# Edge ranges packed two blocks to a register load, fewer register loads before the counting stage, and the number of earlier groups carried in registers

## The reference, cut to what matters

```python
src, dst = edges sorted by dst            # 21250 of them, 1250 nodes of 512 features
neigh = segment_sum(x[src], dst, 1250)    # layer 0: sum over the edges of each node
rst   = (1 + eps) * x + neigh
h     = relu(rst @ W1 + b1) @ W2 + b2 + x
x     = layernorm(x + h)
# then four blocks of attention over the same edges, each with conditional
# layernorms and a two-layer MLP; and a last layernorm
```

## Time and profile before

| | before |
|---|---|
| median of 3 runs | 1729.66 us (1729.47 to 1729.7) |
| the profiled execution's own time | 1729.81 us |
| its span (first to last instruction) | 1728.1 us |
| PE busy | 1708.2 us, 99% |
| start of the first count product | 15.36 us |
| start of the second group's products | 19.65 us |
| end of the counting stage | about 127.4 us |

### The profile page before, as it was taken

How to read it: one execution, slowest core, us unless ns; L and a number is a source line. 1 busy time by engine, 2 the same in 40 slices (tenths; PEclk the granted TensorE clock), 3 DMA queues, 4 the chain that set the end, 5 groups by cost and what they waited for, 6 DMA issues and landing times.

```text
span 1728.1 us, 32350 instructions
## 1 busy us (share of the span) xinstructions
PE 1708.2 (99%) x11894; PEld 1511.2 (87%) x11894; DVE 1214.8 (70%) x2229; ACT 802.9 (46%) x1325; POOL 555.1 (32%) x880
## 2 busy tenths in 40 slices
PE   8999999999999999999999999999999999999998
PEld 7998788889999888889998888899988888999887
DVE  7996559457786875477878673677776835778676
ACT  5668332136665331256663412466644123666531
POOL 1002613312334732023337340133363401333473
PEclk9999999999999999999999999999999999999999
DMA  4003311311111303121113122111131312112222
GB/s 136 1 1 150 116 49 44 127 71 40 47 59 38 96 32 129 40 67 45 47 32 105 48 89 80 47 46 62 32 100 36 109 41 79 34 46 62 70 92 73
DMA packets 64779, 113.08 MB, mean 65 GB/s; under 512 B 15318, under 2 KB 25686, under 8 KB 64640
## 3 DMA queue, kind: packets, MB, share of 16 engines
q1 hardware_dynamic: 64640, 111.22, 19.7%
HBM read 89.19 MB, written 22.00 MB: 64 GB/s over the span
## 4 chain that ended last, share of the span: by engine, by line
PE 98%; DVE 1%; issue 0%; DVEq 0%; DMA 0%; SPq 0%; ACT 0%; POOLq 0%; POOL 0%; ACTq 0%
PE ps L1565 61%; PE ps L1625 16%; PE ps L1720 7%; PE ps L1512 6%; PE ps L1542 3%; PE ps L1652 2%; PE ps L1666 2%; DVE masked_s L1272 1%; PE ps L1482 0%; DVEq L426 0%; PE ps L1581 0%; DMA idx_rows<-in_dst_dram 0%; PE ps L1576 0%; PE ps L1463 0%; DVE hot L1097 0%
## 5 line engine op out<-in xcount | busy, mean ns | idle before, releaser
L1256 DVE TENSOR_TENSOR pT<-ps,pT 128x640 fp32r<-128x640 f32 (+1 forms) x320 | 243.9, 804 | 153.9 <-ACT pT L1016 153.8
L1565 PE MATMUL ps<-yT,w 128*128 128x512 f32 (+1 forms) x1728 | 330.0, 352 | 0.0
L1016 ACT CAST pT<-ps 128x640 fp32r<-128x640 f32 (+1 forms) x320 | 202.4, 685 | 252.9 <-PE ps L1720 247.1
L1565 PEld LDWEIGHTS ps<-yT,w 128*128 128x128 f32 x1728 | 280.6, 189 | 44.8
L1565 PE MATMUL ps<-kh,q_parts 128*128 128x512 f32 (+3 forms) x1440 | 310.5, 360 | 5.4 <-DVE small L1272 5.4
L1565 PEld LDWEIGHTS ps<-kh,q_parts 128*128 128x128 f32 (+1 forms) x1440 | 243.0, 186 | 51.1 <-issue 3.7
L1565 PE MATMUL ps<-w,kh 128*128 128x512 f32 (+1 forms) x960 | 235.4, 396 | 0.0
L1625 PE MATMUL ps<-pT,v 128*128 128x256 f32 (+3 forms) x1600 | 215.6, 281 | 0.0
L953 ACT ACTIVATE s<-masked_s,small 128x1250 f32 (+1 forms) x156 | 211.2, 1354 | 0.0
L1565 PEld LDWEIGHTS ps<-w,kh 128*128 128x128 f32 (+1 forms) x960 | 173.7, 186 | 38.9 <-DVE q L1283 1.8
L1625 PEld LDWEIGHTS ps<-pT,v 128*128 128x128 f32 (+1 forms) x1600 | 200.3, 190 | 0.0
(11 more groups left out here) (189 smaller groups left out, 2534.4 us busy)
## 6 DMA issues: line engine op xcount, KB each, us to landing
mask<-mask_dram SPq DMA_DIRECT2D x24, 640.0 KB, 5.1
x_spill<-x SPq DMA_DIRECT2D x36, 256.0 KB
x<-x_spill SPq DMA_DIRECT2D x36, 256.0 KB, 4.3
rep<-rec_dram SPq DMA_DIRECT2D x64, 128.0 KB, 3.3
w_raw<-in_L_gnn_m_w_dram SPq DMA_DIRECT2D x8, 1024.0 KB, 6.4
mask_y<-mask_dram SPq DMA_DIRECT2D x12, 640.0 KB, 5.3
mask_dram<-mask_out SPq DMA_DIRECT2D x10, 640.0 KB, 2.9
w_l<-in_L_gnn_W_dram SPq DMA_DIRECT2D x2, 2048.0 KB, 13.5
```

The lines of the kernel that those rows point to most:

```text
L1016: nc.scalar.copy(pT[:, 0, turned_places(gh, half), k * P:k * P + R], turn_bank(half, R)).then_inc(p_high, 1)
L1256: nc.vector.tensor_tensor(pT[:, 1, places, k * P:k * P + R], turn_bank(half, R), pT[:, 0, places, k * P:k * P + R].bitcast(F32), ALU.subtr ...
L1565: mine = mm(to, left(a), right(b), start=first and n == 0, stop=final and n == 2)
```

## The change

Six edits. (1) `table` becomes int16, and one 32-bit register load brings the `first` and `quads` of two blocks; DVE and ACT load one value before the first group and four in one load after it, instead of four and then four and two. (2) The number of earlier groups is no longer computed by a product with a triangular matrix (`earlier`) and packed; each engine adds up the `quads` of the blocks that it has passed. (3) PE loads one value of `group_table` before the first group and two behind that group's products, and takes the largest number of groups from the same packed word. (4) POOL's packing waits for that largest number as well (`most_ready`). (5) ACT's first function-table load happens at the start, and its copies of `edge` wait for each half by itself. (6) The products of the bounds stand behind three tiles of x.

```diff
-        table = sb("table", [1, NT + 1], I32)
+        table = sb("table", [1, NT], mybir.dt.int16)
...
-        FIRST_LOAD, LATER_LOADS = range(0, 4, 4), range(4, NT, 4)
+        def load_edge_tiles(engine, first_pair, pairs):
+
+            _, packed = nc.values_load_multi_w_load_instructions(table[0:1, 2 * first_pair:2 * (first_pair + pairs)].bitcast(I32),
+                                                                 engines=(engine,), min_val=0, max_val=2 ** 30 - 1)
+            return list(packed)
+
+        def edge_tiles(eng, packed, j):
+
+            at = packed[j // 2] >> 16 if j % 2 else packed[j // 2]
+            first = eng.snap(at & (QUADS_AT - 1)).with_bounds(min_val=0, max_val=NE - 1)
+            quads = eng.snap((at >> 8) & 63).with_bounds(min_val=1, max_val=NE // HOT + 1)
+            return first, quads
+
+        def groups_before(eng, before, quads):
+            return eng.snap(before + quads).with_bounds(min_val=0, max_val=NT * (NE // HOT + 1))
...
-            act.wait_ge(consts, 4)
-            act.wait_ge(idx_t, 2)
+            act.wait_ge(consts, 6)
+            nc.scalar.copy(dst_gap[0:1, 0, 0:1], ident[0:1, 0:1])
             for a in range(2):
+                act.wait_ge(idx_t, 1 + 2 * a)
                 nc.scalar.copy(edge[:, a, 0:NE], ps[0:ET, a, 0:NE]).then_inc(edges_ready, 1)
...
-            chain(nc.vector.scalar_tensor_tensor(parts[:, 0, :], parts[:, 1, :], float(QUADS_AT), parts[:, 0, :], ALU.mult, ALU.add))
-            nc.vector.scalar_tensor_tensor(table[:, 0:NT], parts[:, 2, :], float(BEFORE_AT), parts[:, 0, :], ALU.mult, ALU.add).then_inc(tiles_s, 1)
-            chain(nc.vector.tensor_reduce(most[:], parts[:, 1, :], AX.X, ALU.max))
-            nc.vector.tensor_copy(group_table[:, 3:4], most[:]).then_inc(most_ready, 1)
+            nc.vector.scalar_tensor_tensor(table[:], parts[:, 1, :], float(QUADS_AT), parts[:, 0, :],
+                                           ALU.mult, ALU.add).then_inc(tiles_s, 1)
+            dve.wait_ge(groups_clear, 1)
+            nc.vector.tensor_reduce(four_groups[:, NT:NT + 1], parts[:, 1, :], AX.X, ALU.max).then_inc(most_ready, 1)
...
-            packed = load_edge_tiles(mybir.EngineType.DVE, FIRST_LOAD)
+            packed = load_edge_tiles(mybir.EngineType.DVE, 0, 1)
+            before = 0
             for j in range(NT):
-                first, quads, before = edge_tiles(dve, packed[j])
+                first, quads = edge_tiles(dve, packed, j)
                 if j == 0:
-                    hots(j, first, dve.snap(before * HOT))
-                    packed += load_edge_tiles(mybir.EngineType.DVE, LATER_LOADS)
+                    hots(j, first, 0)
+                    packed += load_edge_tiles(mybir.EngineType.DVE, 1, PAIRS - 1)
                 with dve.Fori(1 if j == 0 else 0, quads) as k:
                     hots(j, dve.snap(first + k * HOT), dve.snap((before + k) * HOT))
+                before = groups_before(dve, before, quads)
...
-            for t in range(4):
+            for t in range(3):
                 if t == 2:
                     pe.wait_ge(edges_ready, 2)
                 turn_x(t)
             pe.wait_ge(bounds_ready, 1)
-            for a, (value, onto) in enumerate(((0, ident), (1, ident), (1, earlier))):
-                mine = mm(ps[0:1, 5, a * NT:(a + 1) * NT], bounds[:, value:value + 1], onto[0:NT, 0:NT], start=True, stop=True)
+            for a in range(2):
+                mine = mm(ps[0:1, 5, a * NT:(a + 1) * NT], bounds[:, a:a + 1], ident[0:NT, 0:NT], start=True, stop=True)
...
+            load_groups(0, 1)
             before = 0
             for j in range(NT):
                 quads = pe.snap((fours[j // 4] >> 6 * (j % 4)) & 63).with_bounds(min_val=1, max_val=NE // HOT + 1)
-                count_block(j, j % 2, quads, before)
+                count_block(j, j % 2, quads, before, (lambda: load_groups(1, 2)) if j == 0 else None)
```

More of the change, by code:

```diff
@@ L338, in gnn_kernel @@
         tl_i32 = at("yp", 21504, "tl_i32", [NT, NE], I32)
-        parts = at("yp", 24896, "parts", [1, 3, NT])
-        most = at("yp", 25024, "most", [1, 1])
+        parts = at("yp", 24896, "parts", [1, 2, NT])
         four_groups = at("yp", 25056, "four_groups", [1, 12])
@@ L410, in gnn_kernel @@
         EXACT = 4096
-        CONSTS = 12
-        QUADS_AT, BEFORE_AT = 2 ** 8, 2 ** 14
+        CONSTS = 10
+        QUADS_AT, PAIR_AT = 2 ** 8, 2 ** 16
         TILES_DONE = 9
@@ L417, in x_piece @@
             return x_in_s[n], 32 if n == NG - 1 else 16
-        FIRST_LOAD, LATER_LOADS = range(0, 4, 4), range(4, NT, 4)
[L421 to L436, removed]
+        PAIRS = NT // 2
+        def load_edge_tiles(engine, first_pair, pairs):
[9 more added lines that the diff above has]
+            return eng.snap(before + quads).with_bounds(min_val=0, max_val=NT * (NE // HOT + 1))
         @block.sync
@@ L628, in _ @@
             nc.gpsimd.iota(edge_of_i[:], [[P, 2]], base=0, channel_multiplier=P).then_inc(consts, 1)
[L629 to L632, removed]
             nc.gpsimd.memset(minus_one[:], -1.0).then_inc(consts, 1)
@@ L668, in _ @@
             pool.wait_ge(parts_ready, 1)
+            pool.wait_ge(most_ready, 1)
             pool.sem_inc(passed)
@@ L851, in counts_copy @@
                                ).then_inc(counts_out, 1)
-            packed = load_edge_tiles(mybir.EngineType.Activation, FIRST_LOAD)
+            packed = load_edge_tiles(mybir.EngineType.Activation, 0, 1)
+            before = 0
             for j in range(NT):
-                first, quads, before = edge_tiles(act, packed[j])
+                first, quads = edge_tiles(act, packed, j)
                 dst_hots(j, first, before)
@@ L865, in _ @@
                 nc.scalar.copy(x_high[0:rows(j), j, :], x[0:rows(j), j, :]).then_inc(x_high_done, 1)
-            counts_copy(NT - 1, act.snap(before + quads))
+                before = groups_before(act, before, quads)
+            counts_copy(NT - 1, before)
             def rst_high_part(m, g):
@@ L1489, in _ @@
             pe.wait_ge(bounds_ready, 1)
-            for a, (value, onto) in enumerate(((0, ident), (1, ident), (1, earlier))):
-                mine = mm(ps[0:1, 5, a * NT:(a + 1) * NT], bounds[:, value:value + 1], onto[0:NT, 0:NT], start=True, stop=True)
+            for a in range(2):
+                mine = mm(ps[0:1, 5, a * NT:(a + 1) * NT], bounds[:, a:a + 1], ident[0:NT, 0:NT], start=True, stop=True)
             mine.then_inc(bounds_turned, 1)
-            for t in range(4, NT):
+            for t in range(3, NT):
                 if t == 7:
@@ L1496, in _, with count_block @@
                 turn_x(t)
-            def count_block(j, place, quads, before):
+            def count_block(j, place, quads, before, behind_first=None):
                 pe.wait_ge(counts_out, j + 1)
@@ L1516, in count_block @@
                 quad(before, True)
+                if behind_first:
+                    behind_first()
                 with pe.Fori(1, quads) as k:
@@ L1521, in _, with load_groups @@
             pe.wait_ge(group_step, 6)
-            pe.wait_ge(most_ready, 1)
-            _, fours = nc.values_load_multi_w_load_instructions(group_table[0:1, 0:4], engines=(mybir.EngineType.PE,), min_val=0,
-                                                                max_val=2 ** 24 - 1)
+            fours = []
+            def load_groups(a, n):
+                _, found = nc.values_load_multi_w_load_instructions(group_table[0:1, a:a + n], engines=(mybir.EngineType.PE,),
+                                                                    min_val=0, max_val=2 ** 24 - 1)
+                fours.extend(found)
+            load_groups(0, 1)
             before = 0
```

13 lines of the change are left out of this document (6 added, 7 removed).

## The result

| | before | after |
|---|---|---|
| median | 1729.66 us (1729.47 to 1731.34, 5 runs) | 1756.85 us (1756.66 to 1757.47, 5 runs) |
| profiled execution, its span | 1729.81, 1728.1 us | 1757.47, 1755.2 us |
| first count product | 15.36 us | 14.04 us |
| second group's first and third tile | 19.65, 20.85 us | 16.69, 18.40 us |
| start of the neighbour sums (end of the counting) | 127.29 us | 153.81 us |

The change makes the kernel slower: ratio 1.0157, 95% interval 1.0146 to 1.0168. Forecast were 1751 us, range 1741 to 1765; measured 1756.85.

What follows compares the result with a forecast made beforehand. PE was taken to bound the kernel, with DVE close behind in the counting. Loops +24.4, covered hole -0.3 and start -2.5 gave +21.6 us on 1729.81: forecast 1751 us, range 1741 to 1765.

Steps and rivals of the forecast that it cites:

- 1.84 us for a turn: DVE's counting loop: sequencer time of one turn without any wait, 0.82 plus 1.02 us, against PE's 2.24 us a group.
- Rivals 1 and 2: DVE's added rows cost little, 1732 or 1730 us, 7%; register sums not run in each turn, 1727.3 us, 5%.
- rival 3: PE's clock falls because PE pauses in every turn of the counting: 15 us more, 1767 us, 6%.
- The start: Start of the counting up to the second group's third tile: a gain of 2.5 us, bounds 2.2 and 2.7.
- a whole TENSOR_LOAD, 0.54: DVE's register loads before the second group: one load instruction saved, 0.54 us, besides two values, 0.56 us.
- The loops: DVE's counting loops, blocks two to ten: re-run sum adds 3 to 19 rows a turn at 0.10 us, 24.4 us.
- the hole: PE's single idle gap of 0.3 us in the counting, behind one DVE turn: taken as covered, 0.3 us back.
- X: Time added to each DVE turn by the sum's rows, blocks two to ten: 0.18 to 1.78 us.
- margin of 0.2 from pass to first instruction: Counting loop: DVE's one-hot tile is ready some 0.2 us before PE starts that group, after 1.02 us from pass to instruction.
- the sequencer's 0.40: Counting loop: DVE's turn may grow by 0.40 us before it is longer than PE's 2.24 us.
- The lower bound: Low end of the forecast's own range, from a price of 0.08 us for each added DVE row: 1742 us.
- The early function table is worth nothing: ACT's early load at the start: no gain, since PE waited under 0.05 us for the copies of `edge`.

Runs made afterwards that it cites:

- e1: The changed kernel, but DVE adds up the earlier blocks' groups once between two loops, into a register of its own; 1729.15 us, 0.9997 of the kernel before.
- e3: The changed kernel with three semaphore increments that nobody waits for between DVE's loops of the fifth and sixth block; 1756.45 us.
- e4: The changed kernel with sixteen semaphore increments that nobody waits for ahead of DVE's loop of the second block; 1759.34 us.
- e8: e1 with the int16 table as long in bytes as the old one, which moves only addresses; 1728.30 us.
- e11: The kernel before with its table eight unused words longer, so every later array lies 32 bytes higher; 1730.65 us.
- e6: e1 without ACT's early function-table load (its early copy into dst_gap); 1729.28 us.
- e7: e1 with PE loading all three of its values ahead of the first group; 1729.46 us (one run).
- e5: e1 with the products of the bounds behind four tiles of x again; 1729.86 us.
- e2: The kernel before, but DVE's loops take the number of earlier groups from a sum of loaded values, not the packed word; 1749.61 us.
- e12: The kernel before with small arrays put together in pairs, so the large arrays lie 64 bytes lower; 1729.28 us.

## Why the prediction was right, and where its numbers were off

- **The direction and the cause: right.** DVE's re-run sum makes the turns longer than PE's 2.24 us, and with e1, which takes it out of the loops, the loss of 27 us is gone. The two numbers that it rests on hold as well: 1.84 us for a turn less 0.12 for its long row is the 1.72 measured, and the row's 0.10 us is what e3 gives. Rivals 1 and 2 are out (rows cost 0.09 to 0.10 us, pitch and not printed duration, and the sums are run each turn), rival 3 too: the granted clock stays at 1.00 in every window of the stage.
- **The start: 2.5 us forecast, 2.45 in the trace**, in its bounds and with ACT late as the step had it. The path there was a bit different: PE's x ended at 13.78 and its first product came at 14.04. And the merged register load was not the saving that the step had counted ("a whole TENSOR_LOAD, 0.54"): DVE's one load behind the first group took 0.99 us, the two before it 0.35 and 0.54, ACT's 0.93 against 0.31 and 0.50. DVE was early enough all the same.
- **The loops: 24.4 us forecast (24.1 with the hole given back), 29.0 measured. This is the term that was mis-sized.** By window, for the third to the ninth block: forecast 2.24, 2.42, 2.52, 2.82, 2.92, 3.22, 3.32 us a group, measured 2.35, 2.46, 2.69, 3.06, 3.04, 3.26, 3.72. Missing were two things. First, the loop across a fixed place of the code: shown for the sixth block (1.0 us, e3 and e4), read from the place of the gap in four traces for the ninth (some 1.5 to 2 us, no run has that loop off the place), and 0.3 us for the first crossing, which falls into the fifth block's window (the step into the sixth block takes 3.21 us, and 2.93 in e4). I had seen the hole "behind one DVE turn" and counted it as a thing that would be covered, without asking why that turn was slow; it was the first sign of this. Second, the third block: X is 0.28 there, and my own margin of 0.2 from pass to first instruction was the tighter limit, as I read it, not the sequencer's 0.40. The step took only the latter: 0 forecast, 0.5 us measured (11.74 less 5 x 2.24). Together that is some 3.5 of the 4.9 us; the remainder is spread over the other blocks, and I have not traced it to a row.
- **Not in the forecast at all:** 0.58 us behind the counting, from a table that became 24 bytes shorter (e8 and e11, for the cause; one execution's rest is good to some 0.4 us), and 0.56 us outside of the span (open).
- **What was luck:** the range held, but it was drawn from the price of a row, and that price was right. What missed, 4.9 us in the loops and 1.1 around them, came from things for which no bound stood in the sum; they fell inside because the row's bounds were wide. (The lower bound itself, 0.08 us a row, sums to 1743 and not 1742.)
- **"The early function table is worth nothing": right** (e6), but not for the reason given. The prediction put PE's wait for the copies of `edge` at under 0.05 us, from sixteen products in one piece. The row of the weight loads shows a wait:

```profile
9.24 1.57 PEld L1482 LDWEIGHTS ps<-ident,x 128*128 128x128 f32 x8 [0.44 <-ACT edge L820]
```

From the eighth to the ninth product there are 0.46 us, where the others are 0.21 apart: 0.25 us of waiting, gone in the changed kernel and in e6 alike. So it was the waits for each half of `edge`, not the table, that removed it, and the bounds came 1.29 us sooner (11.15 to 9.86), not 0.98.

- PE's later load of two values: nothing either (e7). The bounds behind three tiles: 0.7 us by e5's median, not clear of the noise.

## What to carry to other kernels

An expression of registers that is carried from loop to loop can be a recipe and not a value: look in the built program whether it is formed inside the body, and if so give it a register of its own between the loops. It need not happen: ACT and PE carry the same sum, and their bodies have 12 and 48 instructions in every block, before and after. They use it once in front of each loop, DVE only inside; that this is what makes the difference is read from the code and not tested. When two engines run within 0.2 us of each other in a loop, the sequencer of the second one counts by the row, 0.10 us here, though no engine's busy time shows it. And ask of every hole, even a single one of 0.3 us, why it is there before you count it as covered.

## What was not expected of the hardware

- **A place in the code.** A loop of DVE that lies across its 198th instruction as built has two gaps of about 0.12 us in every turn, in the kernel before, the changed one, e1, e2 and e4 alike. Where the sequencer bounds, the turn is 0.25 us longer for it; where PE bounds, PE loses 0.2 to 0.3 us in that block and no more. The first passing costs some 0.4 us once. A second such place lies at instruction 329. What lies there no run shows.
- **Addresses.** Moving arrays by 32 or 64 bytes changes the 1600 us of the later layers by +0.77 (e11), -0.73 (e12) and +1.08 us (e8 to e1), with the same instructions there. Nearly all of it is PE's busy time. In e12 most of it stands in one row of the page, the products `ps<-kh,q_parts` (310.5 us before, 309.9 in e12); in e11 several rows move by 0.3 to 0.5 us, one of them the other way.
- **The pace of the first products.** PE's products that turn x follow each other every 0.21 us at first and every 0.11 us later, at a granted clock of 1.00 in all of them. The change of pace came at about 11.3 us in the profile of after and at 13.0 in that of e1:

```profile
10.20:10.90 0.70, 0.70 (x4) 1.00 1.08 337
10.90:11.60 0.70, 0.70 (x7) 1.00 1.05 115
11.60:12.30 0.70, 0.70 (x9) 1.00 0.92 195
```

```profile
10.20:10.90 0.70, 0.70 (x4) 1.00 0.96 311
10.90:11.60 0.70, 0.70 (x5) 1.00 0.58 24
11.60:12.30 0.70, 0.70 (x6) 1.00 0.88 236
12.30:13.00 0.70, 0.70 (x5) 1.00 0.89 334
```

(Windows of PE alone: us, busy and count of products, clock, DMA share, GB/s; the first three rows are after's, the last four e1's.) It moves the end of the turned x by up to 1.2 us between executions (13.4 us in e3, 14.7 in e1) and with it the start of the counting. What sets it no run here shows. It is also why single profiles can't settle half a microsecond of the start.
